# Four-layer token mixer on one core: full fp32 matmuls on pairs of token tiles, four key masks, new engine orders

## The chip, the cores and the metric

The kernel runs on one core of a Trainium2 chip. The metric is the device time of one execution in microseconds. The core has TensorE (PE, with its weight loads PEld), VectorE (DVE), ScalarE (ACT), GpSimd (POOL) and SyncE (SP, which here only issues DMAs). Each engine works through its own list of instructions in the order in which the program gives them, and semaphores tie the lists together.

## The reference

The input is x of shape 16 x 64 x 64 x 64 (image n, row a, column b, channel d). Four residual layers follow one another:

```python
z  = layernorm(layernorm(x)) * ln_w + ln_b
q, k, v = z@Wq, z@Wk, z@Wv           # 8 heads of 16 channels
g  = sigmoid(z@Wg + bg)
att = softmax(einsum('iabhc,jabhc->ijabh', q, k) / 4, axis=1)   # over the 16 images, for each pixel (a, b)
x1 = x + (einsum('ijabh,jabhc->iabhc', att, v) * g) @ Wo + bo
p  = softmax(layernorm(x1) @ router_w + router_b); two best of 8, made to sum to 1
x2 = x1 + sum over those two of p_e * (layernorm(x1) @ expert_w[e] + expert_b[e])
u  = layernorm(x2) @ W_exp.T + b_exp # 64 primary and 64 gating channels
x3 = x2 + (primary * sigmoid(running mean of gating along a)) @ W_con.T + b_con
# last layer: 32 experts each pick 8 tokens of every image, pool them, a small MLP, scattered back
```

All values are fp32. Only the first three layers are touched by the change; the last one needs whole images and runs afterwards.

## The kernel before

The first three layers run as one software pipeline over half columns. A half column is 32 rows a of one column b for all 16 images: 512 tokens, four tiles of 128 tokens (`QT = 4`). There are 128 half columns. In a step ("slot") every engine does one stage of each of some eight half columns: `LAG` says by how many slots a stage trails the load of its half column (scores 2, values 3, experts 4, expansion 5, `scan_out` 7, `pick` 8). The function `slots` runs the first steps unrolled, then a loop over i with two slots in its body (q = 0 and 1), then the rest. The order of the `if runs(...)` blocks in each engine's `step` is the order in which the engine works. A second phase afterwards (not changed in substance) does the last layer.

The stages that the prediction speaks of:

- **Normalization.** VectorE takes mean and variance of each token (`bn_stats`, `bn_aggr`), GpSimd subtracts, raises to the power -1/2 and multiplies (`normalize`). For three of the four normalizations the result is then split: ScalarE rounds it to fp32r (`round_part`, L464) and GpSimd subtracts to get the rest (`second_part`, L387). Value and rest stand side by side in 128 columns, and TensorE transposes them tile by tile (`transposed`, L593), so that rows 0 to 63 hold the rounded values and rows 64 to 127 the rests. An fp32r matmul streams a column in one pass.
- **Projections.** q, gate and k are two fp32r matmuls each, over all 512 tokens (`project`, L608 and L609), against the rounded weights and their rests. v is four matmuls in full fp32 (L670), and its bias is added on GpSimd (L406). The expansion (L720, L721) is like q.
- **Keys.** ScalarE writes k eight times, once per head, each copy masked to the 16 channels of its head (`masked_keys`, L472, 128 x 512 each), into `kT`.
- **Scores.** 32 full fp32 matmuls (L640) of 128 rows, 32 weight columns (tokens) and 128 moving columns (8 heads x 16 images), on four column tiles of the array. `kT` is single, so ScalarE may write the next keys only after the scores are done, and the scores wait for the last key copy.
- **Softmax and values.** VectorE takes maxima, differences, sums (L852), a reciprocal and `own_den` (L857). ScalarE does the exponential, GpSimd the product `probs` (L414). VectorE transposes it. 64 matmuls on 32 x 32 tiles (L658) give the values, VectorE gates them (`ogT`, L839), and `att_out` (L687) projects them.
- **Experts.** For each of the four token tiles: a bias matmul of three rows in bf16 (L622) and two fp32r matmuls of 512 columns (L623, L624). VectorE multiplies by the gates (`yg`, L912 and L932, four times 128 x 512), sums over the experts (`mixed`, L811) and adds `x1` (L827).
- **PSUM.** There are eight banks. Two (`shared`) go round by `TURNS`; the scores have one of `s_bank`, k the other; the values have `o_bank`; `BORROWED` lends banks out.
- **DMAs.** SyncE issues 24 in a slot: eight loads of x, eight stores of x3 and eight of its normalized form n3.

The trace has two records for each matmul in full fp32, and one for a matmul in fp32r or bf16 and for a transpose.

## Time and profile before

| | |
|---|---|
| median of 3 runs | 3134.03 us (3119.96 to 3137.24) |
| profiled execution, its own time | 3123.18 us |
| span of its trace | 3121.5 us |
| mean granted TensorE clock | 0.839 of full |
| PE busy | 2647.5 us (85%) |
| DVE busy | 2551.6 us (82%) |
| POOL busy | 2161.0 us (69%) |
| ACT busy | 2005.1 us (64%) |
| PEld busy | 1969.9 us (63%) |
| DMA over the span | 34 GB/s |

Busy is the time in which an engine had an instruction under way. The pipeline over half columns fills the first nine tenths of the span, and the shares are even all along it, so the table is nearly a picture of its steady state. Busy time of PE counts the latency of its last matmul too. A record is marked with the program's name for what it writes and reads, and a line: L593 is line 593.

### The profile page before, as it was taken

To read this page: it belongs to the slowest core of one execution; us is meant where nothing else is said; L and a number is where in the kernel's file an instruction comes from. 1 tells how busy PE (TensorE), PEld (TensorE's weight loads), DVE (VectorE), ACT (ScalarE), POOL (GpSimd) and SP (SyncE) were. 2 spreads that over 40 slices of the span, in tenths; PEclk is the share of its full clock that TensorE was granted. 3 is DMA by queue.
4 is the path that set the end of the run, shared out by engine and by line. 5 is a ranking of instruction groups with operands and counts; after the bars stand their busy time and mean duration, and the time that the engine had idled before them with its cause. 6 is when DMAs were issued, how large, how long until landed. Compare 5 with 4: busy or idle time off the path is not lost. (4 is left out here: it accounts for less than half of the span.)

```text
span 3121.5 us, 108500 instructions
## 1 busy us (share of the span) xinstructions
PE 2647.5 (85%) x37071; PEld 1969.9 (63%) x37071; DVE 2551.6 (82%) x9002; ACT 2005.1 (64%) x3590; POOL 2161.0 (69%) x2963
## 2 busy tenths in 40 slices
PE   2898898888888888898898898888988988896697
PEld 2666666666666656666666666666666666664586
DVE  2788889888888898888888888888889888885604
ACT  2666767766676676776776766677667676762600
POOL 2677777877777777777787877778777777863000
PEclk9788988887888888888887987889889788885858
DMA  0011101111011010110101111011010010101828
GB/s 17 9 20 18 19 17 19 19 18 19 17 19 18 18 19 17 19 19 18 19 17 18 19 18 19 17 19 19 18 19 18 17 19 18 19 15 19 269 96 337
DMA packets 263153, 106.67 MB, mean 34 GB/s; under 512 B 250257, under 2 KB 254900, under 8 KB 258997
## 3 DMA queue, kind: packets, MB, share of 16 engines
q1 hardware_dynamic: 260933, 93.16, 12.9%
q10 hardware_dynamic: 2160, 12.68, 1.0%
q8 instruction: 40, 0.66, 0.1%
q14 instruction: 20, 0.16, 0.0%
HBM read 55.31 MB, written 50.33 MB: 34 GB/s over the span
## 5 line engine op out<-in xcount | busy, mean ns | idle before, releaser
L472 ACT ACTIVATE kT<-s_bank,b_k,block_of 128x512 f32<-128x512 f32 x1024 | 748.8, 771 | 3.6 <-PE s_bank L609 0.3
L640 PE MATMUL s_bank<-kT,qT 128*32 128x128 f32 x8192 | 396.1, 372 | 187.3 <-issue 187.3
L640 PEld LDWEIGHTS s_bank<-kT,qT 128*32 128x32 f32 x8192 | 349.5, 152 | 226.8 <-issue 224.7
L489 ACT ACTIVATE qT<-shared,b_qkg 128x256 f32<-128x256 f32 x256 | 107.5, 471 | 412.0 <-PE shared L609 412.0
L811 DVE TENSOR_REDUCE mixed<-yg 128x256 f32<-128x2048 f32 x128 | 288.5, 2254 | 0.2
L687 PEld LDWEIGHTS o_bank<-w_o,ogT 128*128 128x128 f32 x2048 | 247.9, 193 | 23.7 <-DVE ogT L839 14.8
L414 POOL TENSOR_TENSOR probs<-weights,own_den 128x1024 f32<-128x1024 f32 x128 | 252.7, 1975 | 1.8 <-DVE own_den L857 1.8
L687 PE MATMUL o_bank<-w_o,ogT 128*128 128x64 f32 x2048 | 246.9, 274 | 4.3 <-DVE ogT L839 3.9
L387 POOL TENSOR_TENSOR split_ffn<-norm_ffn,split_ffn 128x256 fp32r<-128x256 f32 x128 | 93.6, 731 | 215.1 <-ACT split_ffn L464 215.1
L658 PEld LDWEIGHTS o_bank<-probsT,v_sb 32*32 32x32 f32 x16384 | 170.2, 107 | 63.7 <-issue 58.1
L658 PE MATMUL o_bank<-probsT,v_sb 32*32 32x64 f32 x16384 | 196.5, 234 | 1.5 <-DVE yg L932 1.5
L387 POOL TENSOR_TENSOR split_att<-norm_att,split_att 128x256 fp32r<-128x256 f32 x128 | 94.0, 735 | 147.4 <-ACT split_att L464 147.4
L622 PE MATMUL shared<-bias,ones 3*128 3x512 bf16 x256 | 109.3, 427 | 98.3 <-ACT picks L532 52.2
L555 ACT ACTIVATE gpre<-shared,bgate_col 64x256 f32<-64x256 f32 x256 | 181.4, 709 | 13.3 <-PE shared L721 10.3
L593 PE MATMUL shared<-ident,split_att 128*128 128x128 f32 x512 | 111.6, 357 | 69.3 <-ACT prim L555 47.9
L377 POOL TENSOR_TENSOR rstd_ffn<-rstd_ffn,minus_half 128x4 f32<-128x4 f32 x128 | 160.1, 1251 | 10.7
L406 POOL TENSOR_TENSOR v_sb<-v_sb,bv_rows 128x512 f32<-128x512 f32 x128 | 163.1, 1274 | 3.0 <-ACT v_sb L504 3.0
L839 DVE TENSOR_TENSOR ogT<-o_bank,gT 128x512 f32<-128x512 f32 x256 | 163.2, 679 | 1.5 <-PE o_bank L658 1.2
L918 DVE STREAM_TRANSPOSE probsT<-probs 128x1024 f32<-128x1024 f32 x128 | 157.9, 1234 | 2.0 <-POOL probs L414 2.0
L593 PEld LDWEIGHTS shared<-ident,split_att 128*128 128x128 f32 x512 | 78.4, 182 | 123.3 <-issue 68.2
L800 DVE SCALAR_TENSOR_TENSOR gated<-ema_t,prim 64x256 f32<-64x256 f32 x256 | 150.3, 587 | 6.8 <-ACT ema_t L564 1.1
L677 PE MATMUL shared<-w_con,gated 128*128 128x64 f32 x1024 | 141.8, 283 | 7.9 <-DVE gated L800 5.8
(204 smaller groups left out, 7648.6 us busy)
## 6 DMA issues: line engine op xcount, KB each, us to landing
x_in<-in_x SPq DMA_DIRECT2D x1024, 16.0 KB, 1.7
x_scratch<-x SPq DMA_DIRECT2D x1024, 16.0 KB, 1.4
normalized_x_scratch<-norm_pick SPq DMA_DIRECT2D x1024, 16.0 KB, 1.5
xa<-normalized_x_scratch SPq DMA_DIRECT2D x16, 1024.0 KB, 8.1
xb<-x_scratch ACTq DMA_DIRECT2D x8, 1024.0 KB, 10.3
out_x<-xa SPq DMA_DIRECT2D x16, 512.0 KB, 5.3
out_x<-xb SPq DMA_DIRECT2D x16, 512.0 KB, 6.9
xa<-x_scratch SPq DMA_DIRECT2D x4, 1024.0 KB, 6.5
```

The source lines that it names most:

```text
L377: ch.link(g.tensor_tensor(r[:, 1, :], r[:, 0, :], minus_half[:], ALU.pow))
L387: g.tensor_tensor(split[kind][z][:, :, 1, :], norm[kind][z][:], split[kind][z][:, :, 0, :].bitcast(F32), ALU.subtract).then_inc(s_split[ki ...
L406: g.tensor_tensor(v_sb[z][:], v_sb[z][:], bv_rows[:].unsqueeze(1).broadcast_to([P, QT, HC]), ALU.add).then_inc(s_v, 1)
L414: g.tensor_tensor(probs[:], weights[:].unsqueeze(2).broadcast_to([P, 32, 2, 16]), own_den[:].unsqueeze(3).broadcast_to([P, 32, 2, 16]), AL ...
L472: ins = s.activation(kT[:, h, :], bk("k")[:], ACT.Identity, bias=b_k[:, h:h + 1], scale=block_of[:, h:h + 1])
L555: ins = s.activation(dst, src, ACT.Identity, bias=bias[r0:r0 + D], scale=scale)
L593: ins = t_.transpose(bank_of(q, name)[:, t * P:(t + 1) * P], split[kind][par(q, lag)][:, t].rearrange("p k d -> p (k d)").bitcast(F32), id ...
L640: ins = t_.matmul(s_bank[g * 32:(g + 1) * 32, 0, t * P:(t + 1) * P], qT[z][:, c, tok:tok + 32], kT[:, :, tok + c * N:tok + (c + 1) * N], s ...
L658: ins = t_.matmul(o_bank[k * 32:(k + 1) * 32, g, t * 64:(t + 1) * 64], v_sb[z][g * 32:(g + 1) * 32, t, k * 32:(k + 1) * 32], pT[g * 32:(g ...
L687: ins = t_.matmul(bk("att_out")[:, t * D:(t + 1) * D], ogT[:, h, tile(t)], w_o2[:, h, :], start=(h == 0), stop=(h == 1))
L811: v.tensor_reduce(mixed[:], yg[:], AX.X, ALU.add).then_inc(s_mixed, 1)
L839: ins = v.tensor_tensor(by_group(ogT[:, h, :]), o, by_group(gT[z][:]), ALU.mult)
```

## The change

Each of the three split normalizations loses its split. The normalized tokens are now laid out as two pairs of token tiles (`norm` is 128 x 2 x 2 x 64), and one transpose turns a pair: rows 0 to 63 of the result hold the channels of one token tile, rows 64 to 127 those of the other. Every projection is a matmul in full fp32 of 64 rows and 256 columns for each half, at array rows 0 and 64 (`tile_position`), into two banks. The four expert tiles are done as two pairs in the same way. v and the experts get their biases by matmuls of three bf16 rows at each half. Keys are masked four times, to 32 channels each (two heads), and the scores take 64 matmuls of 64 rows and 64 columns, one half for each set of four heads. `own_den` and the sum `x2` move from VectorE to GpSimd. VectorE gates two expert tiles at a time. The n3 stores become 16 DMAs of half the size in a slot, so SyncE issues 32. All eight banks are shared out by a table `BANK`, and the order of work on every engine is new.

```diff
-LAG = {"att_t": 1, "k": 1, "q": 1, "gate": 1, "v": 1, "scores": 2,
-       "values": 3, "att_out": 3, "ffn_t": 4, "route": 4, "y0": 4, "y1": 4, "y2": 4, "y3": 4,
...
+LAG = {name: lag for lag, names in STAGES.items() for name in names.split()}
+TURNS = ["att_out", "v", "gate", "scores", "conv_t", "y1", "y0", "expand", "values", "ffn_t", "pick_t", "route",
+         "pick", "att_t", "q", "scan_out", "k"]
+BANK = {"att_out": (1,), "v": (0, 1), "gate": (2, 3), "scores": (4, 5), "conv_t": (3,), "y1": (0, 1), "y0": (2, 3),
+         "expand": (0, 1), "values": (4, 5, 6, 7), "ffn_t": (3,), "pick_t": (0,), "route": (2, 3), "pick": (0, 1),
+         "att_t": (2,), "q": (2, 3), "scan_out": (0,), "k": (2, 3)}
...
-            norm = {k: cpair(f"norm_{k}", [P, QT, D]) for k in KINDS}
-            split = {k: cpair(f"split_{k}", [P, QT, 2, D], F32R) for k in KINDS[:3]}
+            norm = {k: cpair(f"norm_{k}", [P, 2, 2, D]) for k in KINDS}
...
-            kT = cb("kT", [P, H, QTOK])
+            kT = cb("kT", [P, 4, QTOK])
...
+                            for pr in range(2):
+                                sp.dma_start(n3_cols[p, z, column(i, q, "n3st")][:, pr::2],
+                                             norm["pick"][z][p * N:(p + 1) * N, pr]).then_inc(s_n3_store[z], 16)
...
-                def second_part(kind, i, q, lag):
-
-                    z = par(q, lag)
-                    pool.wait_ge(s_hi[kind], at(i, q, lag))
-                    g.tensor_tensor(split[kind][z][:, :, 1, :], norm[kind][z][:], split[kind][z][:, :, 0, :].bitcast(F32),
-                                    ALU.subtract).then_inc(s_split[kind], 1)
...
+                    if runs(i, q, "own"):
+                        pool.wait_ge(s_rden, at(i, q, "own"))
+                        g.tensor_tensor(own_den[:], ssum[:].unsqueeze(2).broadcast_to([P, 32, 2]),
+                                        odd_even[:].unsqueeze(1).broadcast_to([P, 32, 2]), ALU.mult).then_inc(s_own, 1)
...
+                    if runs(i, q, "x2"):
+                        z = par(q, "x2")
+                        pool.wait_ge(s_mixed, at(i, q, "x2"))
+                        g.tensor_tensor(x2[z][:], mixed[:], x1[z][:], ALU.add).then_inc(s_x2, 1)
...
                     def masked_keys(heads):
                         for h in heads:
-                            ins = s.activation(kT[:, h, :], bk("k")[:], ACT.Identity, bias=b_k[:, h:h + 1],
-                                               scale=block_of[:, h:h + 1])
+                            ins = s.activation(kT[:, h, :].rearrange("p (t f) -> p t f", t=2), bk("k")[:, :, 0:2 * P], ACT.Identity,
+                                               bias=b_k[:, h:h + 1], scale=quarter[:, h:h + 1])
                         return ins
...
+                    if runs(i, q, "km0"):
+                        act.wait_ge(filled["k"], at(i, q, "km0"))
+                        wait(act, s_scores, at(i, q, "km0", 1))
+                        masked_keys(range(0, 2)).then_inc(s_half_keys, 1)
+                    if runs(i, q, "km1"):
+                        act.wait_ge(filled["k"], at(i, q, "km1"))
+                        wait(act, s_scores, at(i, q, "km1", 1))
+                        masked_keys(range(2, 4)).then_inc(drained["k"], 1)
...
-                        t_.matmul(bk(name)[:], w_qkg_hi[:, w, :], zT[z1][:], start=True, stop=False)
-                        t_.matmul(bk(name)[:], w_qkg_lo[:, w, :], zT[z1][:], start=False, stop=True).then_inc(filled[name], 1)
...
-                        t_.matmul(bk(y)[:], ones3[:], bias3[:], start=True, stop=False)
-                        t_.matmul(bk(y)[:], tT[z4][:, tile(t)], w_expert_hi[:], start=False, stop=False)
-                        t_.matmul(bk(y)[:], tT[z4][:, tile(t)], w_expert_lo[:], start=False, stop=True).then_inc(filled[y], 1)
...
+                    def projected(name, weights_, moving):
+                        for t2 in range(2):
+                            ins = t_.matmul(bk(name)[:, t2, 0:2 * P], weights_[half_rows(t2)], moving[half_rows(t2)],
+                                            tile_position=(t2 * D, 0))
+                        ins.then_inc(filled[name], 1)
+
+                    def transposed(name, kind):
+                        for p in range(2):
+                            ins = t_.transpose(bk(name)[:, pair_cols(p)],
+                                               norm[kind][par(q, name)][:, p].rearrange("q t d -> q (t d)"), ident[:])
+                        ins.then_inc(filled[name], 1)
+
+                    def experts(p):
+                        y, z = f"y{p}", par(q, f"y{p}")
+                        bank_free(pe, i, q, y)
+                        pe.wait_ge(drained["ffn_t"], at(i, q, y))
+                        for t2 in range(2):
+                            t_.matmul(bk(y)[:, t2], ones3[t2 * D:t2 * D + 3], bias3[t2 * D:t2 * D + 3], start=True, stop=False,
+                                      tile_position=(t2 * D, 0))
+                        for t2 in range(2):
+                            ins = t_.matmul(bk(y)[:, t2], tT[z][half_rows(t2), pair_cols(p)],
+                                            w_expert_ce[half_rows(t2)].rearrange("d c e -> d (c e)"), start=False, stop=True,
+                                            tile_position=(t2 * D, 0))
+                        ins.then_inc(filled[y], 1)
+
...
+                        for t2 in range(2):
+                            t_.matmul(bk("v")[:, t2, 0:2 * HC], ones3[t2 * D:t2 * D + 3], bv3[t2 * D:t2 * D + 3], start=True, stop=False,
+                                      tile_position=(t2 * D, 0))
+                        for p in range(2):
+                            for t2 in range(2):
+                                ins = t_.matmul(bk("v")[:, t2, pair_cols(p)], zT[z][half_rows(t2), pair_cols(p)], w_scaled[half_rows(t2), 3, :],
+                                                start=False, stop=(p == 1), tile_position=(t2 * D, 0))
+                        ins.then_inc(filled["v"], 1)
+                    if runs(i, q, "gate"):
+                        bank_free(pe, i, q, "gate")
+                        pe.wait_ge(drained["att_t"], at(i, q, "gate"))
+                        projected("gate", w_scaled[:, 2, :], zT[par(q, "gate")])
...
                         for t in range(QT):
                             for c in range(2):
                                 for g in range(4):
-                                    tok = t * P + g * 32
-                                    ins = t_.matmul(s_bank[g * 32:(g + 1) * 32, 0, t * P:(t + 1) * P],
-                                                    qT[z][:, c, tok:tok + 32], kT[:, :, tok + c * N:tok + (c + 1) * N],
-                                                    start=(c == 0), stop=(c == 1), tile_position=(0, g * 32))
+                                    for u in range(2):
+                                        tok, rows = t * P + g * 32, slice(u * D, (u + 1) * D)
+                                        ins = t_.matmul(o_bank[g * 32:(g + 1) * 32, u, t * D:(t + 1) * D],
+                                                        qT[z][rows, c, tok:tok + 32],
+                                                        kT[rows, :, tok + c * N:tok + (c + 1) * N],
+                                                        start=(c == 0), stop=(c == 1), tile_position=(u * D, g * 32))
                         ins.then_inc(s_scores, 1)
...
+                        v.tensor_tensor(by_pair(yg[:].rearrange("p t d e -> p t (d e)")).rearrange("p t (d e) -> p t d e", e=NE),
+                                        bk(y).rearrange("p t (d e) -> p t d e", e=NE),
+                                        by_pair(gates[:]).unsqueeze(2).broadcast_to([P, 2, D, NE]),
+                                        ALU.mult).then_inc(drained[y], 1)
```


On TensorE, around the experts, this stood before (tile 0, the expansion, tile 1; `tT` is the transposed input of the experts, `cT` that of the expansion):

```order
L622 MATMUL shared<-bias,ones 128x512 [waits drained_pick]
L623 MATMUL shared<-w_expert_hi,tT 128x512
L624 MATMUL shared<-w_expert_lo,tT 128x512
L720 MATMUL shared<-cT,w_expand_hi 128x512 [waits drained_conv_t]
L721 MATMUL shared<-cT,w_expand_lo 128x512
L622 MATMUL s_bank<-bias,ones 128x512 [waits scores_read]
L623 MATMUL s_bank<-w_expert_hi,tT 128x512
L624 MATMUL s_bank<-w_expert_lo,tT 128x512
```


and this stands there now, one pair of token tiles (banks 0 and 1), the other pair (banks 2 and 3) and the expansion:

```order
L621 MATMUL shared<-bias,ones 128x512 [waits drained_ffn_t,drained_v]
L621 MATMUL shared<-bias,ones 128x512
L624 MATMUL shared<-w_expert_ce,tT 128x512 x2
L621 MATMUL shared<-bias,ones 128x512 [waits drained_ffn_t,drained_conv_t,drained_gate]
L621 MATMUL shared<-bias,ones 128x512
L624 MATMUL shared<-w_expert_ce,tT 128x512 x2
L606 MATMUL shared<-cT,w_expand 128x256 [waits drained_conv_t,drained_y1]
L606 MATMUL shared<-cT,w_expand 128x256
```


The expansion moved behind both pairs, each bias and each product is issued once for array rows 0 and once for rows 64, and the waits on the scores' and the values' readers are gone from here.

On VectorE, from the sum `x3` (written `x` from `x_bc`) to the sum `x1` (written `x` from `x_bo`), this stood before:

```order
L848 TENSOR_TENSOR x<-shared,x_bc 128x256 [waits normalized_pick]
L852 TENSOR_REDUCE ssum<-weights 128x32 [waits exp_done]
L257 REGISTER_ALU
L854 RECIPROCAL ssum<-ssum 128x32 [waits exp_summed]
L857 TENSOR_TENSOR own_den<-ssum,odd_even 128x64 [waits exp_summed]
L800 SCALAR_TENSOR_TENSOR gated<-ema_t,prim 64x32x8 [waits filled_scan_out,ema_tanh]
L800 SCALAR_TENSOR_TENSOR gated<-ema_t,prim 64x32x8
L868 TENSOR_TENSOR x<-o_bank,x_bo 128x256 [waits normalized_ffn,x2_done,x_bo_done,filled_att_out]
L777 BN_STATS bn_ffn<-x 128x6 [waits drained_att_out]
```


and this stands there now, from the sum over the exponentials to `x1` and the statistics of the next load:

```order
L941 TENSOR_REDUCE ssum<-weights 128x32 [waits own_denominators,exp_done]
L944 REGISTER_ALU
L217 REGISTER_ALU [waits x2_bc_done,filled_scan_out]
L948 TENSOR_TENSOR x<-shared,x_bc 128x256 [waits centered_pick,x3_stored0]
L951 COPY top<-top 128x4x2 [waits top_found]
L956 BN_AGGR mv_conv<-bn_conv 128x2 [waits normalized_conv,stats_conv,pool_setup]
L956 BN_AGGR mv_conv<-bn_conv 128x2 x3
L809 RECIPROCAL ssum<-ssum 128x32 [waits exp_summed]
L813 MATCH_REPLACE marked<-top,lg 128x8 [waits top_two,pool_setup]
L813 MATCH_REPLACE marked<-top,lg 128x8 x3
L821 TENSOR_TENSOR x<-shared,x_bo 128x256 [waits centered_ffn,x2_done,x_bo_done,filled_att_out]
L826 BN_STATS bn_att<-x_in 128x6 [waits x_loaded1]
```


The sum `x1`, which waits for `att_out` of TensorE, now comes after the reciprocal and the marking of the two best experts of the next slot, `own_den` is gone from here, and statistics and their aggregates no longer follow one another directly.

## Rows read from the trace of the kernel before

**Rows 1.** View of stages, the steady loop; busy us of each engine, PE clock, DMA

```profile
...
110.00:2852.00 2742.00, 2410.89 (x34610) 1759.58 (x34610) 2409.14 (x8747) 1899.67 (x3436) 2110.31 (x2880) 0.85 0.10 18
...
```

**Rows 2.** View of one line: the sum over eight experts, once a half column

```profile
...
L811 DVE TENSOR_REDUCE mixed<-yg x128: 2249/2253/2286, 110.2 to 2852.3; 128x256 f32<-128x2048 f32 x128
...
```

**Rows 3.** Who waited for whom, 1000 to 2000 us: us in total, times, longest

```profile
...
ACT qT L489 <- PE shared L609: 151.5, 47, 4.2
...
PE s_bank L640 <- issue: 61.6, 41, 2.5
...
```

**Rows 4.** Instructions of ScalarE in order: start, us, operation, idle before it

```profile
...
1519.22 0.84 ACT L489 ACTIVATE qT<-shared,b_qkg 128x256 f32<-128x256 f32 x2 [3.04 <-PE shared L609]
...
1535.80 0.76 ACT L472 ACTIVATE kT<-s_bank,b_k,block_of 128x512 f32<-128x512 f32 x1
...
1541.49 0.84 ACT L489 ACTIVATE qT<-shared,b_qkg 128x256 f32<-128x256 f32 x2 [4.16 <-PE shared L609]
...
```

**Rows 5.** Instructions of TensorE in order: start, us, operation, records

```profile
...
1509.19 0.60 PE L622 MATMUL s_bank<-bias,ones 3*128 3x512 bf16 x1
...
1510.88 0.60 PE L622 MATMUL o_bank<-bias,ones 3*128 3x512 bf16 x1
...
1518.45 0.50 PE L608 MATMUL shared<-zT,w_qkg_hi 128*128 128x512 f32 x1
...
1519.11 1.47 PE L658 MATMUL o_bank<-probsT,v_sb 32*32 32x64 f32 x128
...
1521.01 1.06 PE L670 MATMUL shared<-w_scaled,zT 128*128 128x128 f32 x8
1521.92 1.10 PE L677 MATMUL shared<-w_con,gated 128*128 128x64 f32 x8
...
1523.38 0.40 PE L608 MATMUL s_bank<-zT,w_qkg_hi 128*128 128x512 f32 x1
...
1523.85 1.89 PE L687 MATMUL o_bank<-w_o,ogT 128*128 128x64 f32 x16
...
1530.07 0.39 PE L622 MATMUL s_bank<-bias,ones 3*128 3x512 bf16 x1
...
1531.06 0.38 PE L622 MATMUL o_bank<-bias,ones 3*128 3x512 bf16 x1
...
1536.66 3.64 PE L640 MATMUL s_bank<-kT,qT 128*32 128x128 f32 x64 [2.44 <-issue]
1540.23 0.80 PE L608 MATMUL shared<-zT,w_qkg_hi 128*128 128x512 f32 x1
...
```

**Rows 6.** TensorE in the closing phase: full fp32, 256 columns, two records each

```profile
...
3062.46 3.73 PE L1150 MATMUL o_bank<-eo,picks 128*128 128x256 f32 x16
...
```

**Rows 7.** View of stages around those matmuls, with the granted clock

```profile
...
3060.00:3070.00 10.00, 10.00 (x46) 10.00 (x46) 5.49 (x8) 0.00 (x0) 0.00 (x0) 1.00 0.95 363
...
```

**Rows 8.** Groups by line and shape, 1000 to 2000 us: busy us, mean ns, idle

```profile
...
L472 ACT ACTIVATE kT<-s_bank,b_k,block_of 128x512 f32<-128x512 f32 x368 | 269.4, 771 | 1.2
...
L414 POOL TENSOR_TENSOR probs<-weights,own_den 128x1024 f32<-128x1024 f32 x46 | 90.9, 1977 | 0.0
...
L406 POOL TENSOR_TENSOR v_sb<-v_sb,bv_rows 128x512 f32<-128x512 f32 x46 | 58.6, 1273 | 0.0
...
L387 POOL TENSOR_TENSOR split_att<-norm_att,split_att 128x256 fp32r<-128x256 f32 x47 | 34.5, 734 | 54.0 <-ACT split_att L464 54.0
...
L912 DVE TENSOR_TENSOR yg<-shared,gates 128x512 f32<-128x512 f32 x46 | 31.8, 691 | 1.6
...
L852 DVE TENSOR_REDUCE ssum<-weights 128x32 f32<-128x512 f32 x46 | 31.1, 676 | 0.0
...
L827 DVE TENSOR_TENSOR x<-mixed,x 128x256 f32<-128x256 f32 x47 | 26.4, 561 | 0.0
...
L857 DVE TENSOR_TENSOR own_den<-ssum,odd_even 128x64 f32<-128x64 f32 x46 | 24.3, 527 | 1.6
...
```

**Rows 9.** SyncE's queue: eight stores issued one after another

```profile
...
1502.49 3.81 SPq L326 DMA_DIRECT2D x_scratch<-x  x8
...
```

980 lines of the change are left out of this document (513 added, 467 removed).

## Prediction

> **What bounds the kernel now.** I began with the view of stages, to see which part of the span counts. The sum over the experts runs once in each half column, 128 times from 110.2 to 2852.3 us [rows 2]. That is 127 steps in 2742 us, so one half column takes 21.6 us. The same stretch gives the busy time of each engine in a step, when its sums are divided by 127 [rows 1]: PE 18.98, DVE 18.97, ACT 14.96, POOL 16.62 us. No engine is full. Each of the two busiest stands still for 2.6 us of the 21.6. So there is a ring of waits, and the next view, who waited for whom, shows it: ScalarE waits for the second q matmul (L609) 47 times in 1000 us, that is in every step, 151.5 us in all or 3.3 us a step, and TensorE stands before the scores (L640) for up to 2.5 us [rows 3].
>
> The order in time closes the ring. ScalarE starts `qT` at 1519.22, and goes on without a long pause to the last key copy, 1535.80 to 1536.56. TensorE starts the scores at 1536.66 and the q matmuls at 1540.23, and ScalarE starts its next `qT` at 1541.49 [rows 4, 5]. This turn took 22.3 us: 17.3 on ScalarE, 3.6 for the scores, 1.3 for the q matmuls and hand-overs. ScalarE cannot write keys while the scores read them, and TensorE cannot score before the last key. The kernel is bound by ScalarE and two pieces of TensorE in turn, though both have idle time.
>
> **The change, engine by engine, for one half column.** Prices are those of the groups by line and shape, unless another view is named.
>
> *ScalarE.* Four of eight key copies go, at 0.771 us [rows 8]: 14.96 - 3.08 = 11.9, and the three roundings go as well. The scores now need only half of the keys in a late position. The ring above shrinks by over 3 us, below what other engines need, so it stops being the bound.
>
> *GpSimd.* Three subtractions of 0.735 and the v bias of 1.273 go. The sum `x2` comes (0.735, as the subtraction of the same width), and `own_den`: between nothing and the 0.527 that it takes on VectorE; I take 0.3 [rows 8]. 16.62 - 2.21 - 1.27 + 0.74 + 0.3 = 14.2 us.
>
> *VectorE.* `own_den` 0.527 and `x2` 0.561 go. Four expert products of 0.691 become two of twice the width. Their price is not shown. At no gain it is 1.38. By the two reductions, 512 elements in 0.676 and 2048 in 2.253 [rows 2, 8], an element costs 1.03 ns, and 1024 cost 1.20. I take 1.20, since a product of 512 costs almost what the reduction of 512 does: a gain of 0.36. The sum is 18.97 - 0.53 - 0.56 - 0.36 = 17.5 us, at most 17.9. Everything else on VectorE stays in kind and size.
>
> *SyncE.* Eight stores take 3.81 us to issue, 0.48 each [rows 9]. 24 of them are 11.5 us a step, and 32 are 15.4. This stays under VectorE, with 2 us to spare instead of 10.
>
> *TensorE.* Here the price hangs on one question: do two matmuls of 64 rows, at array rows 0 and 64, run side by side? First what one costs. In the closing phase 16 records of 256 columns in full fp32 take 3.73 us, at full clock [rows 6, 7]. That is 0.23 for a record and 0.47 for a matmul. The split pair of 512 columns costs the same 0.47 (1523.38 to 1523.85 for k, [rows 5]). So a projection over two halves of 256 columns costs 0.47 if they run side by side, as now, and 0.93 if one follows the other. For the answer the nearest row is the one for the values: 128 records on 32 x 32 tiles, four row groups and four column groups, in 1.47 us, or 0.0115 for a record [rows 5]. One record of 64 columns should occupy its tile for a quarter of 0.23, 0.058 us. So five are under way at a time, more than column groups alone would give. I take side by side. Then, from neighbouring starts [rows 5]:
> - q, gate, k, expansion: no change.
> - experts: a tile now takes 0.99 (1530.07 to 1531.06), four take 3.96. A pair needs 0.93 for 512 columns in fp32, and 0.33 + 0.1 for the bias and two changes of tile form (the q pair between two other forms takes 0.66, 1518.45 to 1519.11, against 0.47; so about 0.1 for a change). Two pairs: 2.7. Gain 1.25.
> - v: 0.91 now (1521.01 to 1521.92, eight records of 0.114). Four of those pairs plus bias and changes: 0.8. Gain 0.1. The router's matmuls have the same weights loads and no bias: gain 0.45.
> - transposes: 16 become 8, each a record like those of v, 0.114. Gain 0.9.
> - scores: 3.57 in the row at the lower clock. 128 short records on eight tiles lie between 1.47 (the values) and 3.57; I take the middle, 2.5. Gain 1.05.
>
> The sum: 18.98 - 1.25 - 0.1 - 0.45 - 0.9 - 1.05 = 15.2 us.
>
> **The sum.** VectorE at 17.5 is the fullest engine, SyncE 15.4, TensorE 15.2, GpSimd 14.2. The step is VectorE's work and what it still waits. That is not shown for the new order; it lies between nothing and the 2.6 us of now. One wait will stay: `x1` needs `att_out`, which TensorE can begin only after `scan_out` and k, with 1.9 us of its own (1523.85, [rows 5]), and in the new order VectorE reaches `x1` after eight short operations. Other waits for TensorE should shrink, since it has 4 us of room. I take 1.5. A step takes 17.5 + 1.5 = 19.0 us, 2.6 less than now. Over 127 steps that is 330 us. Against the profiled execution's own time, 3123.2 - 330 = 2793. Added at the ends: eight more stores behind the last half column (4 us) and a longer setup chain for the v bias (some 5): 2802. The median of the runs shown is 11 us (0.35%) above the profiled one. I forecast **2810 us**.
>
> **The rivals.**
> - *Row halves do not run side by side* (slower). TensorE then pays 4 x 0.47 for the projections and the expansion. Two expert pairs cost 5.1 (0.47 + 1.87 + 0.2 each), which is 1.1 more than now. v costs 0.35 more, the router is as now, the transposes still save 0.9, the scores nothing. 18.98 + 1.9 + 1.1 + 0.35 - 0.9 = 21.4 us, and with waits of 1.5 to 2.6 the step is 22.9 to 24.0: 3290 to 3430, say **3350 us**. It decides from the point where TensorE's sum passes 20.1. Against it stands the row for the values; for it, that no row shows tiles of 64 rows at both places. Chance 0.10.
> - *Halves overlap in part, and waits stay as they are.* If the two records of one matmul must pass before the first of the next, a pair takes three units and not two. TensorE rises by 4 x 0.23 + 0.93 + 0.46 = 2.3, to 17.5, level with VectorE, and each waits for the other as now: 17.5 + 2.6 to 3.5 = 20.1 to 21.0. **2940 to 3050 us**, chance 0.17. The Trainium skill, "TensorE: Matmul & The Clock Gate" (Part 3, on what overlaps), says that matmuls start and end strictly in program order. By that rule this case would hold, and the result would be some 2990. The trace speaks against such a cost: at one step of 0.058 for each of the 64 value matmuls they would take 3.7 us, and they take 1.47.
> - *TensorE stays at its lower clock level.* The granted clock is 0.85 in the loop [rows 1], so a third of the time is at 1.2 GHz. An expert tile then takes 1.69 instead of 0.99 (1509.19 to 1510.88 against 1530.07 to 1531.06, [rows 5]). With less work TensorE pauses more often. If it stayed low throughout, the column-bound parts (projections 1.9, experts 2.7, v 0.8, transposes 0.9, scores 2.5: 8.8 us) would grow by 1.7: 15.2 + 6.2 = 21.4, so **3120 to 3250 us**. An engine that is late does not pause, though, and should get its clock back. Chance 0.05. The same page of the Trainium skill (Part 1) says that the lower level is the default and activity lifts it; the trace agrees in that both levels occur in every stretch.
> - *SyncE becomes the ring.* It waits for `x_bo`, issues loads, sixteen n3 stores, and then waits for `x3`. If that wait, now covered by 10 us of slack, exceeds what is left, loads come late and VectorE waits for x: a step of 19.5 to 21, **2870 to 3050 us**. Chance 0.06.
> - *Waits nearly vanish*: a step of 17.5 to 18.2, **2620 to 2710 us**. Chance 0.05.
>
> My forecast has 0.57, with a range of its own of 2710 to 2940 (waits of 0.8 to 2.6).
>
> **How the numbers follow.** A difference under 0.5% cannot be told from none in this kernel. Faster hold the forecast (0.57), the partial overlap (0.17), SyncE (0.06) and the vanishing waits (0.05): 0.85. Of the clock case 0.02 fall within 0.5% and 0.03 are slower; 0.01 of the others may end near nothing. Slower: 0.10 + 0.03 less rounding, 0.12; same 0.03. The range of 2690 to 3000 leaves out the slow halves (0.10), the clock (0.05), part of the partial overlap (0.03) and the lowest cases (0.03).
>
> **What the new profile would show.** The sum over the experts (`mixed`) starting every 19 us. VectorE busy for over 90% of the loop, ScalarE near 60%. No long wait of ScalarE for the q matmuls. Pairs at the same line of TensorE starting within some 0.01 us of each other at rows 0 and 64, with an expert pair done in 1.3 us. The largest waits of VectorE at `x1`, at `yg` or at the load. I am wrong if the two halves start a full record apart, if TensorE is busy for 20 us a step, or if VectorE's busy time did not fall to near 17.5.

## The result, and the profile after

The changed kernel takes **3286.68 us** (median of 4, 3285.95 to 3289.97), the kernel before 3131.61 (4 runs, 3119.96 to 3137.24). The ratio is 1.050, with a 95% interval from 1.047 to 1.053: 5% slower, where 2810 us and 10% faster were forecast.

First the view of stages over the steady loop, and the line of the sum over the experts. They answer to [rows 1, 2]; the columns are busy us of PE, PEld, DVE, ACT and POOL, the granted clock, DMA share and GB/s.

```profile
108.00:3014.00 2906.00, 2552.14 (x43736) 1706.50 (x43718) 2076.94 (x8243) 1347.00 (x2563) 1779.29 (x2632) 0.69 0.10 17
...
L895 DVE TENSOR_REDUCE mixed<-yg x128: 2285/2286/2287, 108.2 to 3013.6; 128x256 f32<-128x2048 f32 x128
```

127 steps in 2905.4 us are 22.9 us a step, where it was 21.6. Divided by 127, VectorE is busy for 16.4 us (18.97 before), ScalarE 10.6 (14.96), GpSimd 14.0 (16.62). All three lost the work that they were to lose. TensorE went from 18.98 to 20.1 us, although it has less to do, and the clock from 0.85 to 0.69. The reader should look at the clock first: 0.69 says that TensorE spends some 60% of the loop at the lower of its two levels (1.2 GHz, where 1.00 is 2.4 GHz). VectorE was to be busy for over 90% of the loop and is busy for 71%.

Next TensorE in order of time, nearly one step. It answers to [rows 5].

```profile
1509.94 0.44 PE L612 MATMUL shared<-ident,norm_ffn 128*128 128x128 f32 x2
1511.09 0.44 PE L612 MATMUL shared<-ident,norm_pick 128*128 128x128 f32 x2 [0.71 <-ACT prim L524]
...
1513.57 0.70 PE L606 MATMUL shared<-zT,w_scaled 64*128 64x256 f32 x4 [0.55 <-ACT zT L545]
1514.81 1.94 PE L729 MATMUL shared<-w_con,gated 128*128 128x64 f32 x8 [0.54 <-DVE gated L924]
1516.68 1.23 PE L606 MATMUL shared<-zT,w_scaled 64*128 64x256 f32 x4
1517.84 3.67 PE L634 MATMUL shared<-w_o,ogT 128*128 128x64 f32 x16
...
1527.17 0.61 PE L621 MATMUL shared<-bias,ones 3*128 3x512 bf16 x2
...
1529.72 0.61 PE L621 MATMUL shared<-bias,ones 3*128 3x512 bf16 x2
```

And the granted clock (the column behind the five busy times) in pieces of the same stretch:

```profile
1509.00:1511.00 2.00, 1.38 (x98) 1.05 (x92) 1.97 (x2) 1.96 (x4) 0.00 (x0) 1.00 0.00 0
...
1513.00:1515.00 2.00, 0.91 (x6) 0.55 (x6) 1.96 (x7) 1.88 (x5) 0.95 (x2) 0.91 0.05 12
1515.00:1517.00 2.00, 2.00 (x10) 1.88 (x12) 1.37 (x9) 0.14 (x1) 0.00 (x0) 0.50 0.15 31
...
1529.00:1531.00 2.00, 2.00 (x6) 0.61 (x6) 1.16 (x2) 0.00 (x0) 2.00 (x3) 0.50 0.16 25
1531.00:1533.00 2.00, 2.00 (x65) 1.05 (x64) 1.52 (x3) 0.35 (x1) 1.18 (x2) 0.82 0.00 0
```

From 1509.9 to 1514.8 TensorE does short things (transposes, the router, `pick`, q) with three waits between them: I call this the **thin stretch**. The clock falls at its end, and stays low from `scan_out` until the end of the experts. At the low level `att_out` takes 3.67 us, against 1.89 in the kernel before at the full clock, and an expert pair 2.55 (1527.17 to 1529.72).

What this does to VectorE is seen in who waited for whom (1000 to 2000 us; us in total, times, longest), the answer to [rows 3]:

```profile
POOL norm_conv L360 <- DVE mv_conv L956: 160.5, 44, 4.1
...
DVE x L821 <- PE shared L634: 138.6, 43, 3.4
ACT kT L488 <- PE shared L606: 107.4, 44, 2.8
...
DVE yg L802 <- PE shared L624: 83.8, 59, 2.5
```

ScalarE's wait for q in front of `qT` (151.5 us) is down to 8.7, as forecast. In its place VectorE waits for `att_out` at `x1`, 3.2 us in every step, and 1.9 us for the expert products. Behind `x1` on VectorE stand three of the four statistics, and the normalizations on GpSimd that use them wait with it.

### The profile page after: what moved, and what is told of

Its sections match the earlier page's. It is cut to its first block and busy times, and to the rows that moved or that the text cites. A ratio compares the mean times of both kernels' runs of the same rounds, so it can differ in the third digit from the quotient of the medians.

```text
span 3285.4 us, 129571 instructions
## 1 busy us (share of the span) xinstructions
PE 2784.5 (85%) x46543; PEld 1909.3 (58%) x46543; DVE 2216.9 (67%) x8491; ACT 1437.8 (44%) x2693; POOL 1820.4 (55%) x2706
## 5 line engine op out<-in xcount | busy, mean ns | idle before, releaser
L634 PEld LDWEIGHTS shared<-w_o,ogT 128*128 128x128 f32 x2048 | 446.4, 330 | 81.9 <-issue 81.9
L606 PE MATMUL shared<-zT,w_scaled 64*128 64x256 f32 x1536 | 405.5, 618 | 101.9 <-ACT zT L545 92.8
L488 ACT ACTIVATE kT<-shared,b_k,quarter 128x512 f32<-128x512 f32 x512 | 356.2, 776 | 304.9 <-PE shared L606 304.9
L802 DVE TENSOR_TENSOR yg<-shared,gates 128x1024 f32<-128x1024 f32 x256 | 312.6, 1221 | 248.9 <-PE shared L624 248.9
L634 PE MATMUL shared<-w_o,ogT 128*128 128x64 f32 x2048 | 470.2, 424 | 0.0
L624 PE MATMUL shared<-w_expert_ce,tT 64*128 64x512 f32 x1024 | 372.0, 812 | 0.0
L662 PEld LDWEIGHTS o_bank<-kT,qT 64*32 64x32 f32 x16384 | 232.1, 143 | 83.5 <-issue 83.4
L729 PEld LDWEIGHTS shared<-w_con,gated 128*128 128x128 f32 x1024 | 206.2, 298 | 114.8 <-issue 48.1
L729 PE MATMUL shared<-w_con,gated 128*128 128x64 f32 x1024 | 228.6, 397 | 50.8 <-DVE gated L924 47.5
L606 PEld LDWEIGHTS shared<-zT,w_scaled 64*128 64x128 f32 x1536 | 182.2, 281 | 148.1 <-ACT zT L545 120.1
L662 PE MATMUL o_bank<-kT,qT 64*32 64x64 f32 x16384 | 262.0, 309 | 0.0
```

The costliest lines, as they stand in the source:

```text
L488: ins = s.activation(kT[:, h, :].rearrange("p (t f) -> p t f", t=2), bk("k")[:, :, 0:2 * P], ACT.Identity, bias=b_k[:, h:h + 1], scale=qua ...
L606: ins = t_.matmul(bk(name)[:, t2, 0:2 * P], weights_[half_rows(t2)], moving[half_rows(t2)], tile_position=(t2 * D, 0))
L624: ins = t_.matmul(bk(y)[:, t2], tT[z][half_rows(t2), pair_cols(p)], w_expert_ce[half_rows(t2)].rearrange("d c e -> d (c e)"), start=False, ...
L634: ins = t_.matmul(bk("att_out")[:, t * D:(t + 1) * D], ogT[:, h, pair_cols(t)], w_o2[:, h, :], start=(h == 0), stop=(h == 1))
L662: ins = t_.matmul(o_bank[g * 32:(g + 1) * 32, u, t * D:(t + 1) * D], qT[z][rows, c, tok:tok + 32], kT[rows, :, tok + c * N:tok + (c + 1) * N],
L729: ins = t_.matmul(bk("scan_out")[:, t * D:(t + 1) * D], gated[z][:].rearrange("p a n -> p (a n)")[:, pair_cols(t)], w_con[:])
```

## The experiments

Three theories went into them. Theory **C**: the clock is the whole loss; it falls since the new order gathers TensorE's short pieces and waits in one stretch, right in front of `scan_out`, k and `att_out`. Theory **O**: the order itself costs, `att_out` being last. Theory **H**: the halves of 64 rows bring nothing side by side. The table gives all runs; a step is the time from the first to the last `mixed` through 127, and the clock is that of the profile from 1000 to 2000 us. Ratios are against runs of the kernel before on the same chip.

| run | median us | ratio, 95% | step | clock |
|---|---|---|---|---|
| before | 3131.61 | 1 | 21.6 | 0.85 |
| changed | 3286.68 | 1.050 (1.047 to 1.053) | 22.9 | 0.69 |
| e1: nine fillers | 2857.65 | 0.909 (0.905 to 0.912) | 19.5 | 0.99 |
| e2: `att_out` early | 3351.17 | 1.063 (1.057 to 1.070) | 23.4 | 0.69 |
| e3: half of `att_out` | 2979.74 | 0.948 (0.945 to 0.952) | 20.5 | 0.75 |
| e4: all pairs on rows 0 to 63 | 4599.77 | 1.461 (1.449 to 1.473) | 33.3 | 0.52 |
| e5: fillers on 64 rows | 3190.15 | 1.019 (1.014 to 1.025) | 22.1 | 0.78 |
| e6: fillers in the experts | 3411.67 | 1.090 (1.084 to 1.095) | 23.8 | 0.72 |
| e7: e1 + `att_out` early | 3119.65 | 0.993 (0.989 to 0.998) | 21.2 | 0.89 |
| e8: before + fillers | 3102.37 | 0.992 (0.988 to 0.995) | 21.4 | 0.95 |
| e9: fillers 3, 3, 0 | 2810.57 | 0.895 (0.890 to 0.900) | 19.3 | 0.97 |
| e10: fillers 2, 2, 2 | 2883.71 | 0.920 (0.914 to 0.926) | 19.7 | 0.95 |
| e11: e1, `att_out` before k | 3004.99 | 0.959 (0.953 to 0.965) | 20.5 | 0.90 |
| e12: e11, fillers 3, 3, 1 | 2997.76 | 0.955 (0.950 to 0.961) | 20.7 | 0.89 |
| e13: `lgm`, `sel` moved | 3312.56 | 1.058 (1.053 to 1.063) | 23.1 | 0.68 |
| e14: e13 + fillers 3, 3, 3 | 2740.97 | 0.876 (0.872 to 0.880) | 18.6 | 0.98 |
| e15: e13 + fillers 3, 3, 0 | 2722.37 | 0.870 (0.865 to 0.875) | 18.4 | 0.98 |
| e16: e13 + fillers 4, 4, 0 | **2702.26** | 0.863 (0.859 to 0.867) | 18.3 | 1.00 |
| e17: transposes twice | 3289.80 | 1.052 (1.048 to 1.056) | 22.9 | 0.70 |
| e18: values in the thin stretch | 3523.73 | 1.126 (1.122 to 1.130) | 24.8 | 0.62 |

### e1: is it the clock?

```diff
+                    def filler(bank, n):
+                        for _ in range(n):
+                            t_.matmul(shared[bank // 2][:, bank % 2], fill_w[:], fill_x[:])
...
                         transposed("ffn_t", "ffn")
+                        filler(2, 3)
...
                         transposed("att_t", "att")
+                        filler(3, 3)
...
                         bank_free(pe, i, q, "scan_out")
+                        filler(0, 3)
```

A **filler** is a matmul of 128 rows and 512 columns whose result nobody reads. `fill_w` and `fill_x` are constants in bf16. The banks are free there, and are written anew before anyone reads them.

> Edit: nine filler matmuls a half column on TensorE (bf16, 128x128 by 512 columns, results never read): three behind ffn_t, three behind att_t, three in front of scan_out; nothing else. Theory C (the clock): the changed kernel is slow because the thin stretch from ffn_t to the q projection, short matmuls with waits between, comes right before scan_out, k and att_out, and TensorE does those at its lower level (att_out 3.67 us for 16 records, 213 ns each, against 112 before). Fillers then cost up to 9 x 0.21 to 0.43 us = 1.9 to 3.9 us of a TensorE that stands idle 2.6 us a step, and bring the granted clock of the loop from 0.69 to 0.85 or more and att_out near 1.9 us: a step of 19.5 to 21.5 instead of 22.9, 2850 to 3100 us. Theory O (the order: att_out behind scan_out and k makes VectorE wait at any clock) and theory H (the 64-row form itself costs): more work on TensorE in front of scan_out only lengthens the step by 0 to 3 us: 3290 to 3650 us.

2857.65 us: the changed kernel with more work for TensorE is 13% faster than without, and beats the kernel before by 9%. The view of stages (a piece of the loop, then the whole), and TensorE in order in one step of it:

```profile
1000.00:2000.00 1000.00, 854.95 (x18462) 543.37 (x18514) 913.07 (x3400) 554.22 (x1060) 731.52 (x1080) 0.99 0.12 20
...
110.00:2587.00 2477.00, 2109.12 (x44730) 1335.10 (x44841) 2222.36 (x8243) 1341.38 (x2564) 1782.01 (x2632) 0.97 0.12 20
```

```profile
1507.30 1.00 PE L739 MATMUL shared<-w_con,gated 128*128 128x64 f32 x8
1508.23 0.70 PE L613 MATMUL shared<-zT,w_scaled 64*128 64x256 f32 x4
1508.86 2.00 PE L641 MATMUL shared<-w_o,ogT 128*128 128x64 f32 x16
...
1512.87 1.48 PE L669 MATMUL o_bank<-kT,qT 64*32 64x64 f32 x128
...
1515.32 0.39 PE L628 MATMUL shared<-bias,ones 3*128 3x512 bf16 x2
...
1516.71 0.39 PE L628 MATMUL shared<-bias,ones 3*128 3x512 bf16 x2
```

`scan_out` takes 1.00 us instead of 1.94, `att_out` 2.00 instead of 3.67, an expert pair 1.39 instead of 2.55. The loss is the clock's, as theory C had it, and the others, which expected over 3290 us, do not hold. The second half of C, that the clock falls because the short pieces are gathered in one stretch, is not shown by this run; e6, e17 and e18 bear on it.

### e2: does the order cost, whatever the clock?

The block of `att_out` on TensorE moves, whole, from in front of v to in front of `scan_out`.

> Edit: TensorE's att_out moves from behind k to between the q projection and scan_out, so that x1 on VectorE finds it done; nothing else moves. Theory O (the order): VectorE no longer waits at x1 (138.6 us of 1000, 3.2 us a step), scan_out and k come later by att_out's 3.7 us and make what waits for them (gpre's neighbour x3, the keys) later by less than that: a step of 20.5 to 21.5, 2950 to 3090 us. Theory C (the clock): att_out now starts earlier but runs at the same lower level, 213 ns a record, and the wait at x1 turns into one at x3 for scan_out and one for the keys; a step of 22.4 to 23.4, 3200 to 3350 us. Theory H: no change, 3286.

3351.17 us, at an unchanged clock. The wait at `x1` is gone, and another stands in its place on the same engine, as C had it. Who waited for whom in e2:

```profile
POOL norm_conv L360 <- DVE mv_conv L956: 266.6, 42, 7.5
ACT kT L488 <- PE shared L606: 213.4, 42, 5.6
...
DVE x L948 <- PE shared L729: 135.9, 42, 4.3
```

VectorE now waits 3.2 us a step for `scan_out` (L729) at `x3`, as much as it waited at `x1`. The keys are late too, and so is GpSimd (266.6 us against 160.5 in the changed kernel).

### e3: what is `att_out` worth?

```diff
-                            for h in range(2):
+                            for h in range(1):
                                 ins = t_.matmul(bk("att_out")[:, t * D:(t + 1) * D], ogT[:, h, pair_cols(t)], w_o2[:, h, :],
-                                                start=(h == 0), stop=(h == 1))
+                                                start=True, stop=True)
```

> Edit: att_out sums one of its two halves of channels (4 of 8 matmuls, 8 of 16 records); the other half of the heads' output is left out. This prices the records of 128 columns on the ring. att_out takes 3.67 us now at 213 ns a record. If it lies on the ring that sets the step (theories C and O) the step falls by nearly all of the 1.8 us that go: 22.9 to 21.1 or 21.5, 3060 to 3120 us. If the granted clock falls further with less work in the stretch, part of this is given back. If theory H holds, or the wait at x1 only covers another one, less than 0.5 us a step: 3230 to 3290 us.

2979.74 us: 2.4 us a step for 1.8 us of work, more than any theory had. The clock rose too, from 0.69 to 0.75, and this run cannot say which part of the 2.4 us is its own. That `att_out` lies on the ring it does say: the wait at `x1` fell from 138.6 to 74.3 us of 1000.

### e4: do the halves run side by side?

`half_rows` returns rows 0 to 63 for both halves, and so do the tile positions.

> Edit: all pairs of 64-row matmuls use array rows 0 to 63, so that the second of a pair must follow the first; the second half then works on the first half's data, so the outputs of every second tile are left out. Instructions, sizes and waits stay. Theory H (the halves bring nothing side by side): the same time within 1%, 3255 to 3320 us. If they do run side by side, as the starts 0.003 to 0.007 us apart say, each pair of 256 columns gets 0.47 to 0.9 us longer, an expert pair 0.9 to 1.7, v and the bias 0.5: 4.5 to 8 us more on TensorE in a step, of which 2.6 us are idle now: a step of 25 to 29, 3550 to 4050 us, less if the fuller TensorE is granted a higher clock (theory C allows a step of 23.5 to 25, 3370 to 3550 us).

4599.77 us. The view of stages, and TensorE in order (L729 is `scan_out`, L606 k, L634 `att_out`):

```profile
1000.00:2000.00 1000.00, 960.62 (x10255) 622.45 (x10244) 475.91 (x1943) 321.00 (x609) 420.53 (x618) 0.52 0.07 12
```

```profile
1518.51 1.97 PE L729 MATMUL shared<-w_con,gated 128*128 128x64 f32 x8
1520.41 2.07 PE L606 MATMUL shared<-zT,w_scaled 64*128 64x256 f32 x4
1522.41 3.67 PE L634 MATMUL shared<-w_o,ogT 128*128 128x64 f32 x16
```

At the same low level `scan_out` and `att_out`, which use the whole array, take what they took (1.94 and 3.67), while k takes 2.00 (1520.41 to 1522.41) and not 1.16 (1516.68 to 1517.84). So the pairs do run side by side, and H falls. The starts of a pair in the changed kernel, 0.003 to 0.007 us apart, agree. My range was missed by 550 us: it allowed for a higher clock in the fuller TensorE and not for a lower one. TensorE was busy for 96% of these 1000 us, and was granted 0.52.

### e5 and e6: what kind of filler, and where?

e5 has e1's fillers on 64 rows (`fill_w[r], fill_x[r]`, r being rows 0 to 63 or 64 to 127). e6 has nine full ones, but in `experts`, four in front of y1 and five in front of y0.

> Edit: the nine fillers of e1 at the same three places, of the same length (512 columns, bf16), but on 64 rows instead of 128, so that half of the array stays empty. e1 gave a step of 19.4 us, 2857.65 us and a granted clock of 0.99 in the loop. Theory P (it is TensorE's pauses that cost it the clock): these fillers fill the same pauses, the clock is 0.95 or more and the time 2850 to 2900 us. Theory W (what counts is how much of the array works, as e4 hints, where TensorE was busy 96% of the time and was granted 0.52): half-filled fillers do only part of it: a clock of 0.75 to 0.9, 2950 to 3250 us.

> Edit: nine fillers of e1's kind, but inside the dense stretch of the experts (four in front of y1, five in front of y0) instead of the thin one from ffn_t to scan_out. Theory C with the place as its point (the clock is lost in the thin stretch): the clock still falls at the q projection or scan_out, att_out stays near 213 ns a record, and the fillers add 1.9 us or more: clock 0.70 to 0.80, step 22.9 to 24.5, 3290 to 3500 us. Theory A (it is the average work of TensorE over a whole step that counts, wherever it lies): as e1, 2850 to 2950 us.

The stages of e5, then those of e6:

```profile
1000.00:2000.00 1000.00, 924.23 (x16170) 577.60 (x16168) 773.01 (x2960) 487.36 (x924) 640.95 (x947) 0.78 0.10 18
```

```profile
1000.00:2000.00 1000.00, 898.09 (x15024) 600.77 (x15066) 692.86 (x2736) 451.97 (x859) 595.93 (x882) 0.72 0.10 16
```

e5 streams as many filler columns as e1, in the same places, and gets a clock of 0.78, not 0.99. That is the outcome which theory W forecast. e6 does e1's work in another place and gets 0.72 and a slower kernel: where the work stands counts, and not only how much of it there is. Together with e4 this says that TensorE's busy share is a poor guide to its clock. In three profiles it was busy for 96, 92 and 85% of the time, and was granted 0.52, 0.78 and 0.99.

### e8: is the change worth anything at one clock?

Nine fillers of the same length in the kernel before (their operands are one of its weight tiles and not constants): four before the scores (behind a wait for the bank, ahead of the wait for the keys), two before `scan_out`, three before `conv_t`.

> Edit to the kernel BEFORE the change: nine fillers of the same length (512 columns, 128 rows, one pass): four in front of the scores, where TensorE waits up to 2.5 us, two in front of scan_out, three in front of conv_t's transposes; the results are never read. It asks what the change is worth at one clock. Before, the granted clock was 0.85 in the loop. With 0.95 or more the ring of key copies, scores and q matmuls gets shorter by the scores' part at the lower clock (3.6 us to some 2.5) and the rest stays on ScalarE: a step of 20.3 to 21.2 instead of 21.6, 2960 to 3090 us. Then the changed kernel with fillers (2857.65) is 3.5 to 7.5% faster at one clock, and the prediction's sum was right but for the clock. If before with fillers came to 2860 or less, the change would be worth nothing even at full clock.

3102.37 us, at a clock of 0.95: 0.8% better than before, a little outside what I expected. `qT` still waits for q 115.1 us of 1000 (151.5 before), so ScalarE's ring of key copies is still there. Taken as it stands the ratio is 0.909 / 0.992 = 0.916, the change 8% faster. That is an upper figure, since e8 does not give the kernel before a full clock where its ring needs one. Here are its fillers in front of the scores, and the scores, in two half columns:

```profile
1506.30 2.06 PE L604 MATMUL s_bank<-w_expert_hi 128*128 128x512 f32 x4
1508.28 3.01 PE L645 MATMUL s_bank<-kT,qT 128*32 128x128 f32 x64
...
1527.14 1.17 PE L604 MATMUL s_bank<-w_expert_hi 128*128 128x512 f32 x4
1529.83 1.95 PE L645 MATMUL s_bank<-kT,qT 128*32 128x128 f32 x64 [1.53 <-issue]
```

In the first the clock is 0.50, the fillers last until the scores start, and the last key copy had ended at 1507.32, 0.96 us earlier; in the second the scores wait 1.53 us for the keys. Half column by half column the two kinds take turns (scores from 1314.70 on, 1336.74, 1357.24, 1378.93 and 1400.33). Without the late start, and with scores of 1.9 us each time, two half columns would be up to 2 us shorter. An estimate from these rows: up to 1 us a step less, 127 us in all, so 2975 to 3102 us for the kernel before at the full clock. Against e1's 2857.65 the change is then worth **4 to 8%** at like clocks. Better placed fillers in the kernel before were not tried.

### e9, e10: how many fillers

e9 has three behind `ffn_t`, three behind `att_t`, none before `scan_out`. e10 has two at each place.

> Edit: e1 without the three fillers in front of scan_out (three behind ffn_t and three behind att_t stay). In e1 VectorE waited 53.1 us of 1000 at x1, 1.0 us a step, behind these fillers, scan_out, k and att_out. If six fillers hold the clock, x1 comes up to 0.6 us earlier a step: 18.8 to 19.1, 2780 to 2820 us. If scan_out, k and att_out (128-column records on the whole array, 0.1 us each) do not hold the clock without fillers in front, it falls there and the time lies between e1 and the changed kernel: clock 0.75 to 0.9, 2950 to 3200 us. I lean to the second a little, since without any fillers the clock fell exactly there.

> Edit: e1 with two fillers instead of three at each of the three places. e1 held the clock at 0.99. If six spread fillers are enough: 2800 to 2857 us, clock above 0.95. If the clock needs all nine: falls in part of the steps, clock 0.8 to 0.95, 2880 to 3050 us.

e9 went against the side to which I leaned: the six hold the clock in most steps, and a step is 0.2 us shorter than e1's. The wait at `x1`, which was to shrink, did not (56.7 us of 1000). e10 has as many but holds it in fewer steps, and is 2.6% slower than e9.

### e7, e11, e12: the order again, at the full clock

e7 is e1 with e2's order. e11 is e1 with `att_out` between `scan_out` and k, and e12 the same with one filler before `scan_out`.

> Edit: e1's nine fillers and e2's order together (att_out between the q projection and scan_out). At the full clock att_out is 1.9 us and VectorE waits 53 us of 1000 for it at x1, 1.0 us a step. If the order costs something once the clock is full, the step falls from 19.4 to 18.5 or 19.0: 2740 to 2810 us. If scan_out and the keys, late by att_out's 1.9 us, turn into the new wait, as in e2 (3351 against 3287): 2860 to 2960 us. I lean to the second, 2890.

> Edit: e1's nine fillers, and att_out moved in front of k (behind scan_out), so that x1 finds it 0.6 us earlier and the keys come 1.9 us later, where e1 shows 4 us from k's end to the scores and two key copies of 0.8 us in them. This asks whether the order costs something once the clock is full. If the clock holds: the wait at x1 (1.0 us a step) shrinks to 0.4: a step of 18.8 to 19.2, 2780 to 2830 us. If the keys become late: 19.4 to 20.5, 2857 to 3000 us. If the order moves the fall of the clock: as e7, 2950 to 3120 us.

> Edit: as e11, with one filler instead of three in front of scan_out. If e11's order is good and seven fillers hold the clock: x1 another 0.4 us earlier, a step of 18.4 to 18.9, 2720 to 2790 us, the shortest of all. If the clock falls: 2900 to 3150 us.

All three lost time against e1, by 5 to 9%, and e7 more than I thought likely; its ten executions also lie further apart than those of any other version (3078.95 to 3187.82 us). e11 shows how: TensorE and its clock around the fall.

```profile
1502.94 0.72 PE L645 MATMUL shared<-w_scaled,zT 64*128 64x128 f32 x8
1505.58 0.70 PE L613 MATMUL shared<-zT,w_scaled 64*128 64x256 f32 x4 [1.92 <-ACT kT L491]
1506.21 1.93 PE L661 MATMUL o_bank<-kT,qT 64*32 64x64 f32 x128
```

```profile
1504.00:1506.00 2.00, 0.42 (x4) 0.30 (x4) 0.60 (x5) 1.64 (x4) 2.00 (x2) 1.00 0.10 17
1506.00:1508.00 2.00, 2.00 (x132) 1.69 (x128) 2.00 (x20) 1.16 (x2) 0.99 (x4) 0.63 0.10 16
```

The wait at `x1` is gone, but k came later, ScalarE copies the keys later, and the gate projection waits 1.92 us for its bank. Behind that wait the clock falls, in nearly every step. Whether these orders would win if the new wait were filled as well was not tried.

### e13 to e16: what is VectorE's busy time made of?

At the full clock VectorE is busy 91% of e1, so it looks like the bound. These rows of the groups by line and shape (x count, busy us, mean ns) say otherwise. First the changed kernel, then e1, then e14:

```profile
L831 DVE TENSOR_TENSOR lgm<-lg,top 128x32 f32<-128x32 f32 x43 | 11.5, 269 | 0.0
...
L841 DVE SCALAR_TENSOR_TENSOR sel<-marked,lge 128x32 f32<-128x32 f32 x43 | 7.7, 180 | 0.0
```

```profile
L841 DVE TENSOR_TENSOR lgm<-lg,top 128x32 f32<-128x32 f32 x52 | 53.7, 1033 | 0.0
L851 DVE SCALAR_TENSOR_TENSOR sel<-marked,lge 128x32 f32<-128x32 f32 x52 | 41.7, 802 | 0.0
```

```profile
L828 DVE TENSOR_TENSOR lgm<-lg,top 128x32 f32<-128x32 f32 x54 | 10.1, 187 | 0.0
...
L875 DVE SCALAR_TENSOR_TENSOR sel<-marked,lge 128x32 f32<-128x32 f32 x54 | 14.0, 260 | 0.0
```

And e1 in order of time, VectorE first, then GpSimd:

```profile
1511.91 1.89 DVE L841 TENSOR_TENSOR lgm<-lg,top 128x32 f32<-128x32 f32 x1
```

```profile
1511.82 1.93 POOL L382 TENSOR_TENSOR probs<-weights,own_den 128x1024 f32<-128x1024 f32 x1 [0.22 <-POOL own_den L376]
```

`lgm` is 32 elements wide and starts 0.09 us after GpSimd's `probs`. It ends with it, at 1513.80 and 1513.75. The Trainium skill, "SBUF — State Buffer" (Who interferes with whom), says that a VectorE instruction with two inputs in SBUF contends with a GpSimd instruction that reads SBUF, and that the order of issue decides who blocks. The rows agree: `lgm` (two inputs) takes 1.89 us, and the `bn_stats` (one input), of which four run beside GpSimd's next instruction from 1513.72, keep 0.21 us each. The edit moves both out of the way of `probs`:

```diff
+                    if runs(i, q, "lgm"):
...
                     if runs(i, q, "x1"):
...
-                    if runs(i, q, "lgm"):
...
-                    if runs(i, q, "sel"):
...
                     if runs(i, q, "ag_pick"):
...
+                    if runs(i, q, "sel"):
+                        dve.wait_ge(s_marked, at(i, q, "sel"))
+                        dve.wait_ge(s_ratio, at(i, q, "sel"))
+                        v.scalar_tensor_tensor(sel[:], marked[:], TAKEN, lge[:], ALU.is_equal, ALU.mult).then_inc(s_sel, 1)
```

`gden` and `grec`, which work on `sel`, move with it.

> Edit to the changed kernel, no fillers: on VectorE lgm moves in front of x1, and sel, gden, grec and gates move behind the statistics (order: lgm, x1, statistics, aggregates, sel, gden, grec, gates), so that the two instructions that read two tiles of SBUF do not start while GpSimd works on probs. At the low clock VectorE stands idle 6 us a step and these lines take 269 and 180 ns, so theory B (blocked by GpSimd) and theory V (VectorE's own work) both expect little: 3240 to 3300 us. An effect over 1% would mean that the chain of gates lies on the ring.

> Edit: e13's order with e1's nine fillers. Theory B (in e1 lgm and sel wait inside VectorE for GpSimd's probs, 1.4 us a step together): lgm and sel fall to some 0.2 us each, VectorE's busy time to 16.4 us a step, and the step from 19.4 to 18.0 or 18.6: 2670 to 2760 us, if the clock holds. Theory V (the busy time is VectorE's own work, and the step is TensorE's ring through scan_out, k and att_out anyway): 2840 to 2870 us.

> Edit: e13's order with e9's six fillers (e9: 2810.57 us; sel takes 1350 ns there and lgm 184). Theory B: 1.2 us a step less, 2650 to 2730 us if the clock holds. Theory V: 2800 to 2820 us.

> Edit: e13's order with four fillers behind ffn_t, four behind att_t and none in front of scan_out. e9 with three and three fell to the lower clock in some steps (granted clock 0.97 between 1000 and 2000 us). If eight fillers hold it: within 1% of e15 or better, 2640 to 2720 us. If they only delay q and scan_out: 2720 to 2800 us.

Alone, at the low clock, the new order brings nothing (3312.56 against 3286.68, 0.8% more and slightly above the range). With the fillers it brings 3.6% against e1 (0.876 to 0.909) and 2.8% against e9, and the two instructions shrink by 1.4 us together (1033 to 187 ns, 802 to 260). So at the full clock that time was a wait for GpSimd, shown as busy time. The step of e14 is 0.9 us shorter than e1's, not 1.4. One more VectorE instruction may hold such a wait: the scan `ema`, also with two inputs in SBUF, went from 1214 ns in the changed kernel to 1622 in e1 and is at 1564 in e14. It was not moved. e16 is the fastest version, 13.7% under the kernel before. What VectorE still waits in it is named by its waits:

```profile
1000.00:2000.00 1000.00, 897.80 (x19708) 568.96 (x19696) 918.70 (x3607) 588.80 (x1130) 781.14 (x1158) 1.00 0.13 22
```

```profile
DVE x L834 <- PE shared L641: 39.6, 55, 0.8
DVE lg L913 <- PE shared L713: 25.9, 28, 0.9
```

### e17 and e18: did the removed work take the clock, or the order?

e17 issues every transpose twice (`for p in (0, 1, 0, 1)` in `transposed`), so that there are 16 records again. e18 moves the block of the values on TensorE from in front of `ffn_t` to between the router and `pick`. Neither has fillers.

> Edit to the changed kernel: every transpose is issued twice (16 records a half column, as many as before the change, two more in each of ffn_t, pick_t, att_t and conv_t); no fillers. If the removed transposes were what held the clock before: clock 0.80 or more, 3000 to 3150 us. If the order is what counts, and six more records in the thin stretch (some 0.9 us of 128 columns) are too little: clock 0.68 to 0.75 and up to 0.9 us a step more, 3280 to 3420 us. e10's six fillers of 512 columns took 1.3 us at the full clock and did most of the work, so I lean to the second, at 3330.

> Edit to the changed kernel: TensorE does the values (128 records on 32 x 32 tiles, 1.5 us) between the router and pick instead of in front of ffn_t; no fillers, nothing else moves. If the thin stretch is what loses the clock and real work can break it: clock 0.80 or more, and although VectorE gets the values up to 1.7 us later (ogT stands in front of gated and with it of scan_out), 2950 to 3200 us. If the delay of ogT and gated only makes the wait before scan_out longer: clock 0.65 to 0.72, 3350 to 3550 us. I give each one half.

e17 takes 3289.80 us, the time of the changed kernel, at a clock of 0.70: the number of transposes is not what held the clock before, and eight records more cost nothing. e18 is 7% slower than the changed kernel. TensorE in order shows why real work did not fill the gap:

```profile
1521.44 0.44 PE L612 MATMUL shared<-ident,norm_ffn 128*128 128x128 f32 x2 [0.90 <-DVE yg L802]
1523.01 0.44 PE L612 MATMUL shared<-ident,norm_pick 128*128 128x128 f32 x2 [1.12 <-ACT prim L524]
```

Where the values stood TensorE now waits 0.90 us before `ffn_t` and 1.12 before `pick_t` (0.71 before), and the clock is lower still, 0.62. The second of my two cases comes nearest (its clock was 0.65 to 0.72). Moved work leaves a gap where it was; the fillers left none.

## Why the prediction was wrong

**What bounded the kernel before**: right. The wait for q went from 151.5 to 8.7 us of 1000, and ScalarE's ring with it. e8 agrees from the other side: a clock of 0.95 instead of 0.85 brought the kernel before 0.8%.

**ScalarE 11.9, GpSimd 14.2, VectorE 17.5 us**: measured 10.6, 14.0 and 16.4. The roundings were named, but not taken off ScalarE's sum, and that its copies `tT`, `lT`, `zT` and `cT` get half as wide was overlooked. The `yg` pair takes 2 x 1.22, set at 1.20. VectorE's other 1.1 us were not forecast; the copy `top` alone went from 0.40 to 0.16, and most of the rest is not accounted for. `own_den` takes 0.29 on GpSimd, as set; `x2` takes 1.15 there and not 0.74, which GpSimd's `norm_ffn` (0.82 before, 0.61 now) and its power (1.26 and 1.01) about make up.

**Row halves side by side**: right. It is shown by e4.

**TensorE's sum of 15.2 us**: right for the full clock. In e1 (stages 110 to 2587 us: busy 2109.12, through 127) it is 16.6 us, of which the nine fillers take some 2.1 (three in 0.66 to 0.74): 14.5. The expert pair was set at 1.3 and is 1.39; v 0.8 and 0.76; the scores, set at 2.5 between two bounds, take 1.5; the projections, set at 0.47, take 0.63 from start to start. The errors nearly cancel.

**"An engine that is late does not pause, though, and should get its clock back. Chance 0.05"**: this is the step that failed. The rival "TensorE stays at its lower clock level" is what happened, at 0.69 instead of 0.50. The sentence takes an engine that is late for one that never pauses. Each step still has the thin stretch with its three waits (0.71, 0.55 and 0.54 us), since they are waits for ScalarE and VectorE and do not go away when TensorE is late. And e4 shows that not even an engine busy for 96% need have the full clock. I had taken removed work as free time ("other waits for TensorE should shrink, since it has 4 us of room"). The new order has a thin stretch in front of the pieces on the ring; the clock falls behind it, and filling it gave the clock back. The trace of before already held the warning, a clock of 0.85 in a kernel whose TensorE was busy for 88% of the loop, and showed one place where it falls, at the wait of 2.44 us in front of the scores:

```profile
1530.00:1535.00 5.00, 3.72 (x14) 1.58 (x13) 4.68 (x10) 4.92 (x9) 4.67 (x7) 1.00 0.16 33
1535.00:1540.00 5.00, 3.34 (x64) 3.22 (x64) 4.81 (x13) 2.33 (x4) 3.58 (x6) 0.52 0.12 20
```

In the changed kernel no wait in the thin stretch is longer than 0.71 us, and the clock falls all the same. One of my signs of being wrong came true: TensorE is busy for 20.1 us a step.

**The rival's price**: 3120 to 3250 us at the low level throughout. It was too low for another reason as well. It let only column-bound parts grow. `att_out`, with 64 columns and 128 weight columns a record, was held at 1.9 us and takes 3.67 at the low level, and `scan_out` 1.87 (1514.81 to 1516.68) against 0.93 (1507.30 to 1508.23). These two and k are 6.7 us in a row between `gated` and `x1` (1514.81 to 1521.51), against 3.6 at the full clock (1507.30 to 1510.86 in e1).

**The waits, 1.5 us** (between 0.8 and 2.6): VectorE stands idle for 22.9 - 16.4 = 6.5 us a step, and this term, the largest error of the sum, is where the lower clock shows. `x1` behind `att_out` was named as the wait that stays. Its size follows from the clock: 3.2 us a step, and 1.0 in e1 (53.1 us, 52 times). At the full clock VectorE is busy for 17.5 us a step (2222.36 through 127) and idle for 2.0.

**The sum**: 19.0 us a step and 2810 us were forecast; e1, the same kernel at the full clock, gives 19.5 and 2857.65. The time was right to 2%; that the kernel would run at the full clock was not. Part of this agreement is luck: VectorE's 17.5 us in e1 hold 1.4 us of blocked time that I did not foresee, against some 1.1 us less work. TensorE's and GpSimd's errors cancel in the same way, and 4 to 8% at like clocks is less than the 10% that the forecast had. At the ends 9 us were added; what lies outside the first and last `mixed` went from 379.4 to 380.0 us.

**Of the Trainium skill**, "TensorE: Matmul & The Clock Gate": Part 1 (the lower level is the default, activity lifts it) bears on the step that failed. I noted that the trace agreed, and gave the case 0.05. The fillers of e1 agree with it (0.99); being busy alone did not lift the clock in e4 (96%, 0.52). Part 3 (matmuls in strict program order) did not cost what I feared: pairs start 0.003 to 0.007 us apart, and the expert pair at full clock takes 1.39 us.

## What to carry to other kernels

When a change takes work from TensorE, read its granted clock by stretch before counting the gain, and ask what stands behind each thin stretch. Here nine matmuls whose result nobody reads, put into the waits, were 2.1 us of TensorE a step and made the step 3.4 us shorter; moving real work there did not help. Price each piece on the ring at both levels, those with many weight columns too. And when a tiny VectorE instruction has a mean of 1 us, look at what GpSimd was doing: its busy time may be a wait, as it was here.

## What the hardware showed that I had not expected

- TensorE busy for 96% of 1000 us was granted 0.52, with its pairs one after another on half of the rows (e4). Fillers on 64 rows brought 0.78, the same number on 128 rows 0.99 (e5, e1).
- Records with 128 weight columns and 64 moving columns follow the clock nearly in full: 16 of them take 3.67 us at the low level and 2.00 at the full one.
- `lgm`, 32 elements wide, took 1.89 us behind GpSimd's `probs`, and 0.19 us on average away from it.
- In e11 the clock fell behind one wait of 1.92 us, although nine fillers stood elsewhere in the same step.

Still open: why exactly the new order loses a clock that the old one kept for two thirds of the time. The removed transposes are not it (e17), the place of the fillers matters (e6), and half-filled ones give less (e5). The fp32r passes over all 128 rows, which became pairs over 64, were not given back in any run.
